# A new plan of pieces for VectorE in a three-stage image pipeline

## The chip, the cores and the metric

The kernel runs on one core of one Trainium2 chip. The time is device microseconds from start to end of the program, the median of three runs. The engines are TensorE (PE for its matmuls, PEld for its weight loads), VectorE (DVE), ScalarE (ACT), GpSimd (POOL) and SyncE (SP), which issues the transfers of the queue named q1.

## The reference

For 64 images of 64 channels by 64 by 64 pixels the reference computes three blocks, each with a residual.

```python
def reference(x, ...):
    h = _L0_tok_ref(x, ...)                                  # 16 pixels -> 1 token: 8-head attention in a 4x4 patch
    h = h + _L0_attn_ref(_layernorm(h, axis=-1), ...)        # selective scan forwards and backwards, gated
    h = h + _L0_ffn_ref(_layernorm(h, axis=-1), ...)         # product keys, then causal attention over 256 tokens
    return h

# the scan, 16 states for each of 128 channels
def step(h, inp):
    dA_t, dBu_t, c = inp
    h = dA_t * h + dBu_t
    return (h, jnp.einsum('bdn,bn->bd', h, c))

# the product keys: two lists of 64 scores for each of 8 heads
scores, idx = jax.lax.top_k(sim, PK_TOPK)                    # 16 best of each list
score = (scores[0][..., :, None] + scores[1][..., None, :])  # all pairs of the two lists
final_scores, pk_idx = jax.lax.top_k(score, FINAL_TOPK)      # 16 best pairs
k = jnp.einsum('bnhk,bnhkd->bnhd', softmax(final_scores), keys_table[ind])
v = jnp.einsum('bnhk,bnhkd->bnhd', softmax(final_scores), values_table[ind])
```

## The kernel before

Three images are in work at once. Each engine runs one loop body per image, and a body has 56 **slots** (`SLOTS`). In a period the engines do three things side by side: the third stage of image b (sums over the tables and attention), the second stage of image b+1 (product keys) and the first stage of image b+2 (patch attention and scan). The engines are tied by semaphores alone; a slot is a place in each engine's program and has no fixed length.

In every slot PE does the dense sums of image b: the exponents of the slot before (line 913), the count of entries over the limit (907), the product with a tile of the table for the slot two before (890, or 896 from slot 50 on). ACT turns the two into weights (line 1164 for the slot before, 1158 for this one), so PE and ACT hand work to each other once a slot. In the slots of `SUMS` PE adds four gathered groups (926); POOL gathers them from the table by indirect transfers (695) up to six groups ahead.

The attention of image b runs one head in seven slots: stage 0 (slots 0, 7, ..., 49) makes q on PE (940) and first waits for the accumulation of the head before on DVE; stage 2 makes v (949); stage 3 the scores (954 to 957), after which DVE takes the maxima (1731, 1732); stage 4 the exponentials on ACT (1196, 1197); stage 5 the transposes (961) and DVE's reciprocal (1735); stage 6 the output (965 to 967), which DVE adds into `acc` (1742).

All other work is cut into **pieces**, and a table of text says in which slot each engine issues a piece: `FIRST` for the first stage, `SECOND` for the second, `OWN` for what of the second stage runs over into the image's own period. `v.` is DVE, `p.` PE, `a.` ACT. Within a slot an engine issues the dense work, then attention, then the pieces of the second stage, then those of the first. The pieces that matter here:

- `T0` to `T19`, DVE: top 16 of the score lists, five steps for each of four groups of eight lists: maximum (1516), indices (1518), replace (1520), maximum (1522), indices (1524).
- `q0`, `q1`, `q2`, DVE (1392 to 1407): scores of the patch attention. ACT's piece `sc` in slot 20 (1064) waits for `q2`. `pv0` to `pv2` finish the patch attention.
- `L` and `G`: the same list steps on the pairs of scores. `pr0`, `pr1` make the pairs; `wd`, `wx`, `wg`, `wh` the softmax weights; `sel`, `selh` (1642 to 1648) mark the chosen pairs.
- `A`, `re`, `lo`, `e`: moved scores, their split in three parts, and one-hot counts. PE turns the counts (`e`, line 875, 16 matmuls), ACT copies them (1151).
- `R0` to `R9`, DVE (1610, 1613): table rows of one list of chosen pairs; each odd one also writes the rows for POOL (1619, 1621). `wb0` to `wb4` (1723) spread the weights.
- `B0` to `B3` (1465), `sf`, `sb` (1474), `C0` to `C3` (1484, 1485), DVE: the scan in four quarters: input, forward and backward scan, product with C and the first sums. `S0` to `S7`, PE (814): the state sums. S0 and S1 wait for C0, S2 and S3 for C1, and so on. `y` ends the scan.

The numbers behind `STORE_...` are SP's slots for the stores of the split scores.

Of the kernel before, what the change touches and what calls it, by code (L numbers as in the profile page):

```python
# [123 lines left out]
45 v.B3 v.sf3  # L124
46 v.sb3
47 v.C0
48 p.S0 v.C1
49 p.S1
50 p.S2 v.C2
51 p.S3 v.C3  # L130
52 p.S4
53 p.S5
54 p.S6
55 p.S7
56 p.y v.y
# [11 lines left out]
9 v.T0 v.T1  # L147
10 v.T2 v.T3 p.s1 a.s1
11 v.T4 v.T5 p.s2 a.s2
12 v.T6  # L150
13 v.T7 v.T8 p.s3 a.s3
14 v.T9 v.T10
15 v.T11
16 v.T12 v.T13
19 v.T14
20 v.T15 v.T16
23 v.T17 v.T18
24 v.T19 v.cp v.i a.cp
25 v.pr0 v.L0 v.L1
26 v.L2 v.L3  # L160
27 v.wd v.pr1
28 a.wd
29 v.wx v.sel v.A0 v.G0
30 a.ln p.A0 a.hi0
31 v.A1 v.G1
32 v.re0 v.e0 a.mi0
33 v.G2 p.A1 a.hi1
34 v.e1 v.lo0
35 v.G3 v.re1 a.mi1
36 v.lo1 p.e0 a.e0  # L170
37 v.G4 v.e2 p.e1 a.e1
38 v.wg v.e3 p.e2 a.e2
39 a.wg p.e3 a.e3
40 v.wh
41 a.l2
44 v.R2
46 v.R3
47 v.X5 v.wb0
49 v.R4 v.R5
50 v.A2 v.A3  # L180
51 v.selh
52 v.R6 v.R7
53 v.wb1 v.e4 p.A2 a.hi2
54 v.R8 v.re2 a.mi2
55 v.e5 v.lo2 p.e4 a.e4
"""

OWN = """
0 p.e5 a.e5
1 v.R9 v.e6 p.A3 a.hi3  # L190
2 v.re3 v.R0 v.lo3 a.mi3
3 v.e7 p.e6 a.e6
4 v.R1 v.wb2 v.wb3 p.e7 a.e7
10 v.wb4
"""


LOAD_X, STORE_OUT, STORE_2, STORE_3, STORE_0, STORE_BC = 13, 15, 1, 5, 40, 35
LOAD_C = (42, 44, 46, 48)


# [1630 lines left out]
```

## Time and profile before

| | us |
|---|---|
| median of 3 runs | 17549.33 |
| lowest, highest | 17534.83, 17637.0 |
| the profiled execution | 17614.6 |
| its span (first to last instruction) | 17612.8 |

| engine | busy us | share of the span |
|---|---|---|
| PE | 13397.9 | 76% |
| DVE | 10470.6 | 59% |
| POOL | 10063.1 | 57% |
| ACT | 7416.4 | 42% |

The mean granted TensorE clock is 0.823 of full speed. The span is 64 images, so 275 us an image with the fill and the drain in it. No engine is full, and what bounds the kernel changes from slot to slot. A row of the trace gives the start in us, the duration in us, the engine, the line, the operation, the tiles written and read, and in brackets how long the engine was idle before it and what ended that: an engine with its line, "issue" (nothing the profile shows), "remote" (an event that the profile can't place) or a DMA.

### The profile page before, as it was taken

To read this page: it belongs to the slowest core of one execution; us is meant where nothing else is said; L and a number is where in the kernel's file an instruction comes from. 1 tells how busy PE (TensorE), PEld (TensorE's weight loads), DVE (VectorE), ACT (ScalarE), POOL (GpSimd) and SP (SyncE) were. 2 spreads that over 40 slices of the span, in tenths; PEclk is the share of its full clock that TensorE was granted. 3 is DMA by queue.
4 is the path that set the end of the run, shared out by engine and by line. 5 is a ranking of instruction groups with operands and counts; after the bars stand their busy time and mean duration, and the time that the engine had idled before them with its cause. 6 is when DMAs were issued, how large, how long until landed. Compare 5 with 4: busy or idle time off the path is not lost.

```text
span 17612.8 us, 261382 instructions
## 1 busy us (share of the span) xinstructions
PE 13397.9 (76%) x71228; PEld 10390.9 (59%) x71228; DVE 10470.6 (59%) x39940; ACT 7416.4 (42%) x17286; POOL 10063.1 (57%) x9220
## 2 busy tenths in 40 slices
PE   4777777777777777777777778777777777777777
PEld 3656556556565555565656656556556665565565
DVE  6656656566566566565665656656656566566562
ACT  2444444444444444444444444444444444344443
POOL 2555555556556556555555556555655555556565
PEclk6888888888888888888888888888888788788888
DMA  2444434444444344343443444444434444344343
GB/s 80 115 114 113 114 108 115 118 110 119 114 112 118 108 115 122 107 116 109 116 117 107 118 111 120 117 113 116 116 108 117 115 112 116 105 116 122 107 116 95
DMA packets 1643030, 1984.06 MB, mean 113 GB/s; under 512 B 527806, under 2 KB 1129022, under 8 KB 1628990
## 3 DMA queue, kind: packets, MB, share of 16 engines
q1 hardware_dynamic: 1346366, 1359.69, 27.2%
q0 software_dynamic: 294912, 604.57, 13.2%
q8 instruction: 665, 10.90, 0.3%
q14 instruction: 1087, 8.90, 0.2%
HBM read 1898.00 MB, written 65.01 MB: 111 GB/s over the span
## 4 chain that ended last, share of the span: by engine, by line
PE 38%; another core or an unknown queue 20%; DVE 15%; issue 13%; ACT 8%; DMA 4%; SPq 1%; DVEq 0%; ACTq 0%
PE bank L890 9%; PE bank L926 6%; DMA moving<-keyspace 4%; PE bank L913 4%; ACT bank L1158 3%; PE bank L907 3%; PE bank L767 2%; PE bank L814 2%; PE bank L875 2%; ACT weight L1164 2%; PE bank L896 1%; PE bank L949 1%; PE bank L851 1%; DVE decay L1484 1%
## 5 line engine op out<-in xcount | busy, mean ns | idle before, releaser
L695 POOL DMA_INDIRECT gath<-in_table_dram,rowsT x9216 | 10062.9, 1092 | 7503.4 <-PE bank L926 3775.8
L890 PE MATMUL bank<-weight,rowtab 128*128 128x256 f32 x12288 | 3919.7, 450 | 0.0
L1164 ACT ACTIVATE weight<-bank 128x512 f32<-128x512 f32 x3584 | 2129.3, 594 | 2782.6 <-PE bank L913 1536.2
L890 PEld LDWEIGHTS bank<-weight,rowtab 128*128 128x128 f32 x12288 | 2814.0, 230 | 825.2 <-issue 196.6
L926 PEld LDWEIGHTS bank<-spread,gath 128*128 128x128 f32 x18432 | 2868.0, 223 | 202.3 <-issue 14.5
L913 PE MATMUL bank<-moving,pick_b 96*128 96x512 bf16 x3584 | 1583.5, 442 | 1730.9 <-ACT bank L1158 1282.0
L926 PE MATMUL bank<-spread,gath 128*128 128x96 f32 x18432 | 2773.9, 301 | 15.6 <-issue 15.3
L1158 ACT ACTIVATE bank<-bank,seventeen 128x512 f32<-128x512 f32 x3584 | 2379.1, 664 | 545.9 <-issue 408.5
L907 PE MATMUL bank<-moving,pick_b 96*128 96x512 bf16 x3584 | 1590.2, 444 | 420.4 <-DMA moving<-keyspace 256.4
L913 PEld LDWEIGHTS bank<-moving,pick_b 96*128 96x128 bf16 x3584 | 400.9, 112 | 2268.3 <-ACT bank L1158 1545.6
L1731 DVE TENSOR_REDUCE negmax<-bank 128x1 f32<-128x128 f32 x512 | 147.8, 289 | 2601.6 <-remote 1389.4
L1474 DVE TENSOR_TENSOR_SCAN decay<-decay,wide 128x1024 f32<-128x1024 f32 x512 | 1162.8, 2282 | 26.3
L1742 DVE SCALAR_TENSOR_TENSOR acc<-bank,rrow,acc 128x64 f32<-128x64 f32 x1024 | 245.3, 278 | 1553.2 <-issue 1080.4
L814 PE MATMUL bank<-decay,ident 128*128 128x256 f32 x2048 | 680.8, 461 | 506.7 <-DVE decay L1485 479.3
L767 PE MATMUL bank<-wkv,pix 128*128 128x130 f32 x4096 | 724.3, 328 | 379.9 <-issue 269.2
L767 PEld LDWEIGHTS bank<-wkv,pix 128*128 128x128 f32 x4096 | 616.1, 228 | 580.0 <-issue 450.9
L1089 ACT ACTIVATE decay<-delta,a_neg 128x255 f32<-128x255 f32 x2048 | 867.3, 503 | 1.7 <-DVE mx L1459 1.7
L814 PEld LDWEIGHTS bank<-decay,ident 128*128 128x128 f32 x2048 | 413.5, 224 | 619.5 <-DVE decay L1485 492.2
L1516 DVE MAX8 best<-sim 128x8 f32<-128x64 f32 x2048 | 281.6, 209 | 807.9 <-ACT sim L1111 785.2
L1054 ACT ACTIVATE wide<-bank 128x390 f32<-128x390 f32 (+1 forms) x768 | 346.3, 461 | 950.6 <-remote 779.3
L1709 DVE TENSOR_TENSOR onehot<-keys_b,idx_b 128x2048 bf16<-128x2048 bf16 x512 | 621.1, 1213 | 155.4 <-remote 136.5
L907 PEld LDWEIGHTS bank<-moving,pick_b 96*128 96x128 bf16 x3584 | 376.6, 105 | 568.6 <-DMA moving<-keyspace 274.7
(266 smaller groups left out, 20279.7 us busy)
## 6 DMA issues: line engine op xcount, KB each, us to landing
rowtab<-in_tableD_dram SPq DMA_DIRECT2D x2048, 256.0 KB
wide<-states SPq DMA_DIRECT2D x512, 512.0 KB
moving<-keyspace SPq DMA_DIRECT2D x3072, 64.0 KB
gath<-in_table_dram,rowsT POOLq DMA_INDIRECT x9216
moving<-keyspace SPq DMA_DIRECT2D x3072, 32.0 KB
pix<-in_x_dram SPq DMA_DIRECT2D x64, 1024.0 KB
pix<-in_x_dram SPq DMA_DIRECT2D x128, 512.0 KB
keyspace<-split SPq DMA_DIRECT2D x192, 256.0 KB, 2.0
```

The lines of the kernel that those rows point to most:

```text
L695: pool.indirect_dma_start(out=gath[:, u % RING, j, :], out_offset=None, in_=table, in_offset=bass.IndirectOffsetOnAxis(ap=rowsT[k][:, col: ...
L767: last = mm((scan_ps, misc)[c % 2][:, (n - n0) * KVW:(n - n0 + 1) * KVW], pix[:, n * TOK + t * P:n * TOK + (t + 1) * P], wkv[:], start=Tru ...
L814: mm(scan_ps[:, r * TOK:(r + 1) * TOK], ident[:], decay[r][:, n * TOK:(n + 1) * TOK], start=(n == 0 and r == 0), stop=False, skip_group_ch ...
L890: last = mm(dense_ps[:, 0:TOK], rowtab[:, r, s % 2 * 2 + half, :], weight[s % 2][:, half * TOK:(half + 1) * TOK], start=(s % 16 == 0 and h ...
L907: mm(zd_ps[s % 2][:], pick_b[:, 1, :], moving[r][:], start=True, stop=True, skip_group_check=True).then_inc(over_mm, 1)
L913: mm(zd_ps[s % 2][:], pick_b[:, 0, :], moving[s % KEY_RING][:], start=False, stop=True, skip_group_check=True).then_inc(z_ready, 1)
L926: last = mm(sums_ps[:, col:col + STREAM], gath[:, u % RING, j, :], flat[:, col:col + STREAM], start=True, stop=True)
L1089: last = af(decay[r][:, n * TOK + 1 - r:(n + 1) * TOK - r], delta[:, 1 - r:TOK - r], ACT.Exp, scale=a_neg[:, r * STATE + n:r * STATE + n + 1])
L1158: af(zd_ps[s % 2][:], zd_ps[s % 2][:], ACT.Relu, scale=-BIG, bias=seventeen[:, 0:1]).then_inc(over_ready, 1)
L1164: af(weight[s % 2][:], zd_ps[s % 2][:], ACT.Exp, scale=-1.0).then_inc(weight_ready, 1)
L1474: ins = v.tensor_tensor_scan(d, d, j, 0.0, ALU.mult, ALU.add)
L1709: ins = v.tensor_tensor(hot[:], keys_b[:].unsqueeze(1).to_broadcast([P, 2, KEYS, TOPK]), mine.unsqueeze(2).to_broadcast([P, 2, KEYS, TOPK] ...
```

## The change

Only the tables are changed, so every piece does what it did, in another slot. The diff, cut to the lines spoken of:

```diff
--- before.py
+++ after.py
@@ -124,12 +124,11 @@
 47 v.C0
-48 p.S0 v.C1
-49 p.S1
-50 p.S2 v.C2
-51 p.S3 v.C3
-52 p.S4
-53 p.S5
+48 v.C1
+50 p.S0 p.S1 v.C2
+51 p.S2 v.C3
+52 p.S3
+53 p.S4 p.S5
 54 p.S6
@@ -147,55 +146,55 @@
-19 v.T14
-20 v.T15 v.T16
+17 v.T15
+18 v.T16
+19 v.T17
+20 v.T18 v.T19 v.cp a.cp
...
-49 v.R4 v.R5
-50 v.A2 v.A3
-51 v.selh
-52 v.R6 v.R7
+49 v.wb1
+52 v.e4 v.R8 p.A2 a.hi2
...
-LOAD_X, STORE_OUT, STORE_2, STORE_3, STORE_0, STORE_BC = 13, 15, 1, 5, 40, 35
+LOAD_X, STORE_OUT, STORE_2, STORE_3, STORE_0, STORE_BC = 13, 15, 0, 4, 37, 35
```

All moves, as slots before -> after. DVE: T7 13 -> 12, T9 14 -> 13, T11 15 -> 14, T12 16 -> 15, T14 19 -> 16, T15 20 -> 17, T16 20 -> 18, T17 23 -> 19, T18 23 -> 20, T19 24 -> 20, i 24 -> 21, pr0 25 -> 22, L0 and L1 25 -> 23, L2 and L3 26 -> 24, wd 27 -> 24, pr1 27 -> 25, wx, sel and A0 29 -> 26, G0 29 -> 27, A1 and G1 31 -> 28, re0 and e0 32 -> 29, G2 33 -> 30, e1 and lo0 34 -> 31, G3 and re1 35 -> 32, lo1 36 -> 33, G4 37 -> 33, e2 37 -> 34, wg and e3 38 -> 34, wh 40 -> 36, R2 44 -> 36, R3 46 -> 37, X5 and wb0 47 -> 37, R4 49 -> 38, R5 49 -> 40, A2 50 -> 41, A3 50 -> 42, selh 51 -> 42, R6 52 -> 44, R7 52 -> 46, wb1 53 -> 49, e4 53 -> 52, R8 54 -> 52, re2 54 -> 53, e5 55 -> 53, lo2 55 -> 54, and of the own period R9 1 -> 54, e6 1 -> 55, re3 and R0 2 -> 1, e7 3 -> 2, R1, wb2 and wb3 4 -> 3. PE's and ACT's halves of these pieces move with them: PE's e0 to e3 from slots 36 to 39 to slots 33 to 36, A0 30 -> 27, A1 33 -> 30, A2 53 -> 52, A3 1 -> 0, e4 and e5 one slot forward, e6 and e7 from 3 and 4 to 2 and 3.

Line numbers below and in the changed kernel are one smaller from line 128 on. In the orders that follow a row is line, operation, tile written and tiles read, size, and how often.

On PE, around the first state sums, before (814 are the state sums, 913, 907, 890 the dense work of slot 49, 940 is attention stage 0, which waits for DVE's 1742):

```order
L967 MATMUL bank<-vo,probT 128x64
L809 REGISTER_ALU
L814 MATMUL bank<-decay,ident 128x256 x2
L912 REGISTER_ALU
L913 MATMUL bank<-moving,pick_b 128x512
L907 MATMUL bank<-moving,pick_b 128x512
L890 MATMUL bank<-weight,rowtab 128x256 x2
L940 MATMUL bank<-xT,wq_ffn 64x256
L814 MATMUL bank<-decay,ident 128x256 x2
```

and changed:

```order
L906 MATMUL bank<-moving,pick_b 128x512
L889 MATMUL bank<-weight,rowtab 128x256 x2
L939 MATMUL bank<-xT,wq_ffn 64x256
L911 REGISTER_ALU
L912 MATMUL bank<-moving,pick_b 128x512
L906 MATMUL bank<-moving,pick_b 128x512
L884 REGISTER_ALU
L895 MATMUL bank<-weight,rowtab 128x128 x4
L920 REGISTER_ALU
L925 MATMUL bank<-spread,gath 128x96 x4
L808 REGISTER_ALU
L813 MATMUL bank<-decay,ident 128x256 x4
```

The dense work of slot 49 now stands ahead of the first state sums, and so does attention stage 0; S0 and S1 stand together behind the sums of slot 50.

On DVE, from the accumulation of slot 48 on, before:

```order
L1742 SCALAR_TENSOR_TENSOR acc<-bank,rrow,acc 128x64 x2
L1484 TENSOR_TENSOR decay<-decay,wide 128x1024
L1485 TENSOR_TENSOR decay<-decay 128x512
L1484 TENSOR_TENSOR decay<-decay,wide 128x1024
L1485 TENSOR_TENSOR decay<-decay 128x512
L1610 TENSOR_TENSOR apart<-pair_row,fin_p 128x800
L1613 TENSOR_REDUCE row_f<-apart 128x16
L1610 TENSOR_TENSOR apart<-pair_row,fin_p 128x800
L1613 TENSOR_REDUCE row_f<-apart 128x16
L1619 SCALAR_TENSOR_TENSOR rowx<-row_f,headoff 128x32
L1621 STREAM_TRANSPOSE rowsT<-rowx 128x32
```

and changed:

```order
L1741 SCALAR_TENSOR_TENSOR acc<-bank,rrow,acc 128x64 x2
L1483 TENSOR_TENSOR decay<-decay,wide 128x1024
L1484 TENSOR_TENSOR decay<-decay 128x512
L1483 TENSOR_TENSOR decay<-decay,wide 128x1024
L1484 TENSOR_TENSOR decay<-decay 128x512
L524 REGISTER_ALU
L1722 TENSOR_TENSOR spread<-wT,own 128x256
L1483 TENSOR_TENSOR decay<-decay,wide 128x1024
L1484 TENSOR_TENSOR decay<-decay 128x512
```

The two row pieces R4 and R5 between C1 and C2 are gone from here; they now stand in slots 38 and 40.

On DVE, between the maxima of slot 17 and the end of `q2`, for which ACT waits, before:

```order
L1732 TENSOR_REDUCE negmax<-bank 128x1
L1392 COPY qs<-bank 128x144
L1394 TENSOR_TENSOR decay<-wide,qs 128x2048
L1399 TENSOR_REDUCE sc<-decay 128x256
L1735 RECIPROCAL rrow<-rowsum 128x2
L1524 MAX_INDEX best_i<-best,left 128x8 x8
L1402 TENSOR_TENSOR sc<-sc,rstd 128x256
L1403 TENSOR_TENSOR sc<-sc,qs 128x256
L1406 TENSOR_REDUCE mx<-sc 128x16
L1407 TENSOR_TENSOR sc<-sc,mx 128x256
```

and changed:

```order
L1515 MAX best<-sim 128x8 x8
L1391 COPY qs<-bank 128x144
L1393 TENSOR_TENSOR decay<-wide,qs 128x2048
L1517 MAX_INDEX best_i<-best,sim 128x8 x8
L1398 TENSOR_REDUCE sc<-decay 128x256
L1734 RECIPROCAL rrow<-rowsum 128x2
L1519 MATCH_REPLACE left<-best,sim 128x64 x8
L1401 TENSOR_TENSOR sc<-sc,rstd 128x256
L1402 TENSOR_TENSOR sc<-sc,qs 128x256
L1405 TENSOR_REDUCE mx<-sc 128x16
L1406 TENSOR_TENSOR sc<-sc,mx 128x256
```

Where one list step stood there are three: T15, T16 and T17 in place of T14.

## Rows read from the trace of the kernel before

**Rows 1.** The page's head: span, engines.

```profile
span 17612.8 us, 261382 instructions
PE 13397.9 (76%) x71228; PEld 10390.9 (59%) x71228; DVE 10470.6 (59%) x39940; ACT 7416.4 (42%) x17286; POOL 10063.1 (57%) x9220
```

**Rows 2.** Groups over the whole run: count | busy us, mean ns | idle us before, releasers.

```profile
L814 PE MATMUL bank<-decay,ident 128*128 128x256 f32 x2048 | 680.8, 461 | 506.7 <-DVE decay L1485 479.3 <-issue 26.9
```

**Rows 3.** Stretches, slots 31-38, 38-45, 48-52: length, busy PE PEld DVE ACT POOL, granted clock.

```profile
8067.30:8105.30 38.00, 28.31 (x145) 22.11 (x143) 17.97 (x95) 15.35 (x38) 16.56 (x18) 0.77 0.42 124
8105.30:8133.80 28.50, 24.20 (x137) 19.48 (x136) 22.67 (x24) 21.01 (x53) 22.79 (x17) 0.83 0.53 170
8147.10:8166.30 19.20, 17.97 (x91) 13.29 (x92) 18.62 (x37) 6.40 (x13) 15.55 (x12) 0.86 0.46 116
```

**Rows 4.** Timeline, PE, slots 48 and 49.

```profile
8147.06 2.08 PE L814 MATMUL bank<-decay,ident 128*128 128x256 f32 x4 [6.40 <-DVE decay L1485]
8148.93 0.63 PE L913 MATMUL bank<-moving,pick_b 96*128 96x512 bf16 x1
8151.62 1.05 PE L940 MATMUL bank<-xT,wq_ffn 64*64 64x256 f32 x2
8152.60 1.13 PE L814 MATMUL bank<-decay,ident 128*128 128x256 f32 x4
```

**Rows 5.** Timeline, DVE, the waits of slots 38, 41 and 45, and slot 48.

```profile
8105.27 0.29 DVE L1731 TENSOR_REDUCE negmax<-bank 128x1 f32<-128x128 f32 x1 [7.78 <-PE bank L957]
8117.10 0.48 DVE L1742 SCALAR_TENSOR_TENSOR acc<-bank,rrow,acc 128x64 f32<-128x64 f32 x2 [2.30 <-issue]
8133.77 0.29 DVE L1731 TENSOR_REDUCE negmax<-bank 128x1 f32<-128x128 f32 x1 [2.87 <-PE bank L957]
8146.92 0.47 DVE L1742 SCALAR_TENSOR_TENSOR acc<-bank,rrow,acc 128x64 f32<-128x64 f32 x2
```

**Rows 6.** Groups over the whole run, DVE: the pieces R (two rows), e.

```profile
L1613 DVE TENSOR_REDUCE row_f<-apart 128x16 f32<-128x800 f32 x640 | 630.9, 986 | 22.0
L1610 DVE TENSOR_TENSOR apart<-pair_row,fin_p 128x800 f32<-128x800 f32 x640 | 627.7, 981 | 17.1
L1709 DVE TENSOR_TENSOR onehot<-keys_b,idx_b 128x2048 bf16<-128x2048 bf16 x512 | 621.1, 1213 | 155.4 <-remote 136.5 <-PE bank L875 10.4 <-issue 8.4
```

**Rows 7.** Stretches, DVE busy: slots 38 to C0; A2, A3, selh; wg, wh, X5, wb0.

```profile
8105.20:8147.00 41.80, 35.62 (x43) 0.83 0.55 169
sum 1.94, DVE 1.83; mean DVE 0.92
sum 2.40, DVE 2.20; mean DVE 0.73
```

**Rows 8.** Groups over the whole run: own period and slot 27, ACT.

```profile
L1142 ACT ACTIVATE split_h<-rest 128x128 bf16<-128x128 f32 x64 | 19.8, 310 | 127.9 <-issue 102.6 <-DVE rest L1684 24.9
L1037 ACT ACTIVATE lnv<-var 128x34 f32<-128x34 f32 (+1 forms) x128 | 27.0, 211 | 154.5 <-DVE var L1436 87.1 <-issue 61.2 <-DVE var L1383 6.2
```

**Rows 9.** Groups over the whole run: sc on ACT, the list steps on DVE.

```profile
L1064 ACT ACTIVATE sc<-sc 128x256 f32<-128x256 f32 x64 | 26.6, 416 | 185.7 <-issue 111.8 <-DVE sc L1407 73.9
L1518 DVE FIND_INDEX8 best_i<-best,sim 128x8 uint32<-128x64 f32 x2048 | 411.2, 220 | 117.9 <-issue 117.2
L1516 DVE MAX8 best<-sim 128x8 f32<-128x64 f32 x2048 | 281.6, 209 | 807.9 <-ACT sim L1111 785.2 <-issue 22.8
```

**Rows 10.** Timeline: T16 on DVE (first, last of 16 rows), ACT meanwhile.

```profile
8009.47 0.09 DVE L1518 MATCH_VALUE_LOAD best_i<-best,sim 128x8 f32 x1 [1.25 <-DVE best L1516]
8015.21 0.22 DVE L1518 FIND_INDEX8 best_i<-best,sim 128x8 uint32<-128x64 f32 x1
8015.32 0.38 ACT L1190 ACTIVATE qT<-bank 64x256 f32<-64x256 f32 x1 [7.03 <-remote]
```

**Rows 11.** Groups over the whole run: e2 and e3 on PE; the copies of e on ACT.

```profile
L875 PE MATMUL bank<-down_b,onehot 128*128 128x128 bf16 x2048 | 168.3, 242 | 66.4 <-ACT split L1151 52.1 <-issue 9.4 <-DVE onehot L1709 3.5
L1151 ACT ACTIVATE split<-bank 128x128 bf16<-128x128 f32 x384 | 105.9, 276 | 849.7 <-remote 560.2 <-PE bank L875 248.7 <-issue 38.7
```

More of the change, by code:

```diff
@@ L149 @@
 11 v.T4 v.T5 p.s2 a.s2
[L150 to L154, printed above, removed]
-19 v.T14
-20 v.T15 v.T16
[L157 to L178, printed above, removed]
-49 v.R4 v.R5
-50 v.A2 v.A3
-51 v.selh
-52 v.R6 v.R7
-53 v.wb1 v.e4 p.A2 a.hi2
-54 v.R8 v.re2 a.mi2
-55 v.e5 v.lo2 p.e4 a.e4
+12 v.T6 v.T7
+13 v.T8 v.T9 p.s3 a.s3
+14 v.T10 v.T11
+15 v.T12
+16 v.T13 v.T14
+17 v.T15
+18 v.T16
+19 v.T17
+20 v.T18 v.T19 v.cp a.cp
+21 v.i
+22 v.pr0
+23 v.L0 v.L1
+24 v.L2 v.L3 v.wd
+25 v.pr1 a.wd
+26 v.wx v.sel v.A0
+27 v.G0 a.ln p.A0 a.hi0
+28 v.A1 v.G1
+29 v.re0 v.e0 a.mi0
+30 v.G2 p.A1 a.hi1
+31 v.e1 v.lo0
+32 v.G3 v.re1 a.mi1
+33 v.lo1 v.G4 p.e0 a.e0
+34 v.e2 v.wg v.e3 p.e1 a.e1
+35 a.wg p.e2 a.e2
+36 v.wh v.R2 p.e3 a.e3
+37 v.R3 v.X5 v.wb0 a.l2
+38 v.R4
+40 v.R5
+41 v.A2
+42 v.A3 v.selh
+44 v.R6
+46 v.R7
+49 v.wb1
+52 v.e4 v.R8 p.A2 a.hi2
+53 v.re2 v.e5 a.mi2
+54 v.lo2 v.R9 p.e4 a.e4
+55 v.e6 p.e5 a.e5
 """
 OWN = """
[L189 to L193, printed above, removed]
+0 p.A3 a.hi3
+1 v.re3 v.R0 a.mi3
+2 v.lo3 v.e7 p.e6 a.e6
+3 v.R1 v.wb2 v.wb3 p.e7 a.e7
 10 v.wb4
 """
-LOAD_X, STORE_OUT, STORE_2, STORE_3, STORE_0, STORE_BC = 13, 15, 1, 5, 40, 35
+LOAD_X, STORE_OUT, STORE_2, STORE_3, STORE_0, STORE_BC = 13, 15, 0, 4, 37, 35
 LOAD_C = (42, 44, 46, 48)
```

## The prediction

> **What bounds the kernel now.** I read the page's head first, then the groups with their idle time, then one period by stretches, then its timeline where an engine waits long. The reader is to see in the head that no engine comes near the span [rows 1]: PE 76%, DVE and POOL under 60%. So this is a kernel of hand-overs, and which engine ends a wait last has to be asked place by place. All figures below are us per image unless another unit stands there.
>
> In slots 31 to 38 DVE works 17.97 of 38.00, and PE is busy 28.31; from slot 38 to 45 DVE works 22.67 of 28.50, and from slot 48 to 52 it works 18.62 of 19.20 [rows 3]. DVE is thus the engine waited for from about slot 45 to slot 52 and has room before. The clearest sign is PE's state sum S0: it stands in slot 48 behind C0 and waits 6.40 for it [rows 4]; over the run those waits are 479.3, so 479.3 / 64 = 7.5 an image [rows 2]. POOL's rows and gathers are not waited for there. The second place where DVE is waited for is slot 20: ACT's `sc` sits idle 185.7 / 64 = 2.9 until `q2` is through [rows 9]. Before slot 38 it is the other way round: DVE waits 7.78 for the scores of PE [rows 5].
>
> **The change part by part.** It adds and removes no arithmetic and no transfer; it moves pieces. Six places count, each per image.
>
> 1. *Slots 38 to 47, until C0.* Moved in: R4 to R7, moved out: R2 and R3, so two row pieces more at 0.981 + 0.986 = 1.97 each [rows 6], 3.94, with one more writing of rows, about 0.4. Moved out too is e3, 1.21 [rows 6]. Of the small pieces A2, A3 and selh come in with 1.94, and wg, wh, X5 and wb0 leave with 2.40 [rows 7]. Net 3.94 + 0.4 - 1.21 + 1.94 - 2.40 = +2.7 of DVE work. The stretch is 41.80 long with 35.62 busy [rows 7], so DVE would need 38.3 without a wait. It does wait, in slot 41 for 2.30 and in slot 45 for 2.87 [rows 5], for PE; PE loses e2 and e3 there (168.3 / 64 = 2.6 [rows 11]), so it comes sooner. Bounds: 0 if the waits stay, -3.5 if all go. I take the middle, **-1.7** for the end of C0.
>
> 2. *S0 to slot 50.* In slot 49 PE waits at attention stage 0 for DVE's accumulation of slot 48, which starts in DVE's order right behind C0 (8146.92, against S0's 8147.06) [rows 4, 5]. So the wait does not go, it changes its name. What is won is the dense work of slot 49: from 8148.93 to 8151.62, 2.7, which PE now does inside the wait [rows 4]. Behind the wait the clock was at the lower level: S0 took 2.08 where the next sums took 1.13 [rows 4]. A pause shorter by 2.7 may cost less of this; bounds 0 and -1.6 (the 0.95 of S0 and some 0.65 of the dense work behind it, by the same ratio), I take -0.8. On the other side PE's A3 comes ahead of `y`, +0.4 at most (a piece of 2 matmuls against the 16 of an e, 1.3 [rows 11]). Sum **-3.1**, bounds -4.3 and 0 (0 if DVE, not PE, sets slot 52). DVE would not: of its 18.62 in slots 48 to 52 [rows 3] R4, R5, A2, A3 and selh leave (3.94 + 0.4 + 1.94 = 6.3).
>
> 3. *Own slots 0 to 4.* R9 and e6 no longer stand ahead of re3, for which ACT's split_h waits 127.9 / 64 = 2.0 [rows 8]. Bounds -2.0 and 0; I take **-1.4**, since PE has the same work to do there.
>
> 4. *Slots 17 to 20.* Between the maxima of slot 17 and the end of `q2` there is now T15, T16, T17 instead of T14: a maximum of 281.6 / 256 = 1.1 and an index step of 411.2 / 256 = 1.6 more [rows 9], 2.7 together. `sc` waits already, so this lies on the path whole, unless a later wait swallows it: right behind, in slot 21, ACT stood 7.03 in a wait called "remote" [rows 10]. Bounds 0 and +2.7; I take **+2.0**.
>
> 5. *Slots 24 to 32.* With T19, pr0 and the first lists gone from slots 24 and 25, `h1` comes sooner, and ACT's wait at 1037 (154.5 / 64 = 2.4 [rows 8]) falls by about 1. In slot 32 ACT's copy for side 1 now stands behind G3, ten maxima at the pace of [rows 9], 1.3, and a subtraction: +1.5. Together **+0.5**, bounds -2.4 and +1.7.
>
> 6. *Slots 33 to 38.* e2 and e3 come in from slots 38 and 39: PE 2.6, and each has a copy on ACT of 0.28, which waited 849.7 / 384 = 2.2 [rows 11]. PE and ACT bound this stretch, since DVE waits 7.78 at its end [rows 5]. Some falls into waits that are there. Bounds 0 and +4; I take **+2.0**.
>
> The store slots 37, 0 and 4 follow the pieces; SP has nothing more to issue and waits there for copies one slot old, as before. I put it at nothing; if a copy came late, the key loads behind it would be late next.
>
> The sum is -1.7 - 3.1 - 1.4 + 2.0 + 0.5 + 2.0 = -1.7. Of 64 images some 61 run in the full pipeline, so -104. From the profiled execution, 17614.6, it gives 17511. That execution is 65 over the median of the three runs, 17549.33; taken off the median, which is what I forecast, it is **17445** (-0.6%). All bounds at their low end are -3.5 - 4.3 - 2.0 + 0 - 2.4 + 0 = -12.2, at the high end 0 + 0 + 0 + 2.7 + 1.7 + 4 = +8.4 (16805 and 18062); terms of different places will not all end on one side.
>
> For the clock in part 2, the page "TensorE: Matmul & The Clock Gate" of the Trainium skill (section "What's actually happening") says that the default state is the throttled one and that activity releases it. A pause of 3 to 4 us would stay in front of attention stage 0, and by that rule the work behind it may still be slow. The low clock behind the pause of 6.40 agrees with it [rows 4]. With no gain of clock the sum would be -0.9 an image, 17494.
>
> **The rivals.** *The added work hides.* ACT's waits called "remote" are long: 7.03 before 1190 in slot 21 [rows 10] and 560.2 / 64 = 8.8 an image before the copies of e [rows 11]. If they end at a time that the pieces ahead do not move, then part 4 costs nothing and part 6 only 0.5: -1.7 - 2.0 - 1.5 = -5.2, times 61 = -317, so 17232 (-1.8%). For it speaks their size; against it that I cannot say what they wait for. The page "Runtime: NRT & Kernel Launch" of the Trainium skill (section "Instruction fetch mechanics") has instruction fetch mostly hidden behind running work, which would speak against such waits being fetch; no row here decides.
>
> *Slow lists in front of q2.* T16's index step, 1.6 on average, took from 8009.47 to 8015.21 here, 5.7 plus, because its instructions came in steps of 0.7 [rows 10]. Today this costs little, since `q2` is already through. In the change T16 and T17 stand in front of `q2`. If they keep this pace there, each costs 3.6 more (7.2 together): -1.7 + 7.2 = +5.5, times 61 = +336, so 17885 (+1.9%). It decides from an extra of 4.6 (then +2.9, +1%). Against it: T14, in the very place between q1 and q2, ran quickly, or the wait of `sc` would be longer than 2.9 [rows 9].
>
> *S0's move does nothing.* The wait at attention stage 0 takes all: part 2 is 0, the sum +1.4, +85, so 17634 (+0.5%). The order and the numbers of part 2 speak against it, since the 2.7 of slot 49 does run inside the wait.
>
> **How the numbers follow.** A measurement of this kernel tells about 1% from no change. My forecast, with the likeliest sum, has 0.31. "The added work hides" has 0.25, and I give 0.08 more to gains over 1% from parts 1 and 2 at their better ends. "S0's move does nothing" has 0.14. Slow lists have 0.14, and 0.08 goes to part 6 at its worse end with little won in part 1. So faster by over 1%: 0.33; within 1%: 0.31 + 0.14 = 0.45; slower by over 1%: 0.14 + 0.08 = 0.22. The range reaches from a little below 17232 to between the 17634 of the third case and the 17885 of the second: 17180 to 17780, which leaves out about 0.1 on each side.
>
> **What would show it.** Right: PE's idle time before 814 nearly gone, and in its place a wait of 3 to 4 before 940 in slot 49, ended by DVE's accumulation; DVE's maxima of slot 52 some 4 to 5 sooner after those of slot 38; the wait of split_h below 1; `sc` waiting over 5. Wrong: the wait before 940 as long as the 6.40 of S0 with C0 no sooner (parts 1 and 2); `sc` waiting as before (part 4); T16 or T17 several us long in front of `q2` (the second rival); stretches 31 to 38 longer by over 4 (part 6). The forecast fails altogether if the waits called "remote" grow where the order has changed, for nothing in the rows tells what sets them.

## The result, and the profile after

| | before | after |
|---|---|---|
| median of the runs | 17565.36 us (4 runs) | 18000.25 us (4 runs, 17984.6 to 18028.71) |
| ratio | | 1.0233, 95% interval 1.0214 to 1.0252 |
| profiled execution | 17614.6 us | 17984.6 us |
| one image, slot 0 to slot 0, mean of 59 | 272.0 us | 277.7 us |

The change made the kernel 2.3% slower. The forecast was 0.6% faster, 17445 us, with a range up to 17780: both its sign and its range were wrong. The page of the kernel after, its head and the groups that answer to [rows 1, 2, 8, 9, 11] (lines after 128 are one lower than before):

```profile
span 17982.8 us, 261638 instructions
PE 13440.4 (75%) x71228; PEld 10390.2 (58%) x71228; DVE 10464.2 (58%) x39940; ACT 7441.1 (41%) x17286; POOL 10222.6 (57%) x9220
L813 PE MATMUL bank<-decay,ident 128*128 128x256 f32 x2048 | 608.2, 430 | 114.3 <-DVE decay L1484 80.3 <-issue 32.6
L939 PE MATMUL bank<-xT,wq_ffn 64*64 64x256 f32 x1024 | 383.6, 460 | 551.5 <-DVE acc L1741 450.1 <-issue 101.1
L1141 ACT ACTIVATE split_h<-rest 128x128 bf16<-128x128 f32 x64 | 19.7, 308 | 88.1 <-DVE rest L1683 88.1
L1063 ACT ACTIVATE sc<-sc 128x256 f32<-128x256 f32 x64 | 26.6, 416 | 256.3 <-issue 159.9 <-DVE sc L1406 96.4
L1036 ACT ACTIVATE lnv<-var 128x34 f32<-128x34 f32 (+1 forms) x128 | 26.7, 209 | 11.0 <-DVE var L1382 7.9 <-DVE var L1435 2.8
L1150 ACT ACTIVATE split<-bank 128x128 bf16<-128x128 f32 x384 | 106.4, 277 | 1256.3 <-remote 1013.6 <-PE bank L874 232.9 <-issue 9.8
L694 POOL DMA_INDIRECT gath<-in_table_dram,rowsT x9216 | 10222.4, 1109 | 7714.5 <-PE bank L925 4158.3 <-issue 2631.5 <-remote 685.7
```

No engine has more instructions than before; POOL's 9216 gathers take 10222.4 us instead of 10063.1. PE's idle time before the state sums has nearly gone (506.7 before, 114.3 now), and the wait has its new name at L939, as forecast. Before, that line had read:

```profile
L940 PE MATMUL bank<-xT,wq_ffn 64*64 64x256 f32 x1024 | 375.1, 451 | 241.3 <-issue 151.1 <-DVE acc L1742 83.9 <-remote 5.8
```

What grew is ACT's wait before the copies of `e`, from 849.7 to 1256.3, and within it the part called "remote", from 560.2 to 1013.6.

Where in the image does the time go? The slots are marked by the start of ACT's activation for the count over the limit (L1158, in the changed kernel L1157), one in each slot. The difference of their lengths, after minus before, mean of 59 images, summed from slot 0:

| up to the end of slot | 4 | 16 | 20 | 23 | 32 | 38 | 45 | 48 | 52 | 53 | 54 | 55 |
|---|---|---|---|---|---|---|---|---|---|---|---|---|
| after minus before, us | -0.5 | +1.0 | +2.8 | +1.2 | -0.4 | -3.3 | -5.2 | -11.6 | -6.8 | -3.6 | +5.2 | +5.7 |

By the end of slot 52 the change is 6.8 us an image ahead; the forecast was 1.7 for the whole image. Slots 53 and 54 take 12 us, more than the whole gain. In one image there, by stretches (length, busy PE, PEld, DVE, ACT, POOL with their instructions, granted clock, DMA share, GB/s), the first three beside [rows 3]:

```profile
8226.40:8262.40 36.00, 27.40 (x165) 21.76 (x166) 18.65 (x67) 17.58 (x44) 16.42 (x16) 0.83 0.49 147
8262.40:8288.90 26.50, 20.68 (x116) 16.20 (x116) 25.91 (x36) 19.93 (x47) 21.84 (x14) 0.97 0.46 138
8302.00:8316.20 14.20, 14.20 (x72) 11.36 (x73) 11.10 (x13) 4.11 (x8) 11.77 (x8) 0.78 0.53 145
8316.20:8323.80 7.60, 7.60 (x57) 6.81 (x55) 7.46 (x9) 2.78 (x8) 6.07 (x6) 1.00 0.32 91
8323.80:8344.00 20.20, 8.67 (x36) 5.64 (x34) 2.79 (x7) 1.64 (x3) 13.23 (x14) 0.62 0.19 54
```

In the last stretch PE, DVE and ACT work 8.67, 2.79 and 1.64 us out of 20.20, and the DMA engines are busy 19%. Only POOL goes on, gather after gather. The timeline of POOL, ACT, DVE and PE there:

```profile
8323.76 0.95 POOL L694 DMA_INDIRECT gath<-in_table_dram,rowsT  x1 [0.30 <-issue]
8325.02 0.99 POOL L694 DMA_INDIRECT gath<-in_table_dram,rowsT  x1 [0.31 <-issue]
...
8340.05 0.94 POOL L694 DMA_INDIRECT gath<-in_table_dram,rowsT  x1 [0.30 <-issue]
```

```profile
8325.10 0.66 ACT L1157 ACTIVATE bank<-bank,seventeen 128x512 f32<-128x512 f32 x1
8333.47 0.49 ACT L1200 ACTIVATE probT<-bank 128x384 f32<-128x384 f32 x1 [7.70 <-remote]
8344.06 0.28 ACT L1150 ACTIVATE split<-bank 128x128 bf16<-128x128 f32 x1 [10.10 <-remote]
8344.38 0.47 DVE L1741 SCALAR_TENSOR_TENSOR acc<-bank,rrow,acc 128x64 f32<-128x64 f32 x2 [17.70 <-remote]
```

```profile
8323.27 0.49 PE L960 MATMUL bank<-ident,prob 128*128 128x128 f32 x3
8325.31 0.44 PE L874 MATMUL bank<-ident_b,onehot 128*128 128x128 bf16 x4 [0.33 <-issue]
...
8336.25 0.27 PE L965 MATMUL bank<-vo,probT 128*128 128x64 f32 x1 [0.23 <-issue]
...
8337.66 0.26 PE L966 MATMUL bank<-vo,probT 128*128 128x64 f32 x1 [1.14 <-issue]
...
8344.48 1.90 PE L874 MATMUL bank<-ident_b,onehot 128*128 128x128 bf16 x16 [5.63 <-ACT split L1150]
```

Here the reader is to see three things. ACT's copy `probT` (L1200) needs the transposes of PE's L960, done at 8323.8, and starts at 8333.5; the copy at L1150 needs the sums of e4, done by 8325.8, and starts at 8344.1. So these waits end long after the work that they wait for: that is what "remote" means here. PE meanwhile issues about one matmul every 0.7 us. And all of it starts again 3 us after POOL's last gather of a row of 14, 1.25 us apart (0.94 of work, 0.30 of issue).

Is that one image, or a rule? I call a run of gathers that start under 1.6 us apart a train, and took the busy share of each engine in the 1.2 us behind the start of each gather, by its place in the train (worked out from the records of 59 images):

| place in the train | before: PE, DVE, ACT | after: PE, DVE, ACT |
|---|---|---|
| 1st | 0.82, 0.80, 0.56 | 0.82, 0.84, 0.56 |
| 4th | 0.83, 0.53, 0.27 | 0.83, 0.46, 0.30 |
| 6th | 0.55, 0.29, 0.13 | 0.58, 0.35, 0.17 |
| 8th | 0.42, 0.19, 0.12 | 0.40, 0.11, 0.11 |
| 10th | 0.12, 0.29, 0.07 | 0.16, 0.13, 0.03 |
| 13th | none | 0.09, 0.01, 0.02 |

So the kernel before has it too: trains of 8 or more come 7 times an image there (423 in 59 images), but only 10 of them had over 10 gathers. After the change 53 had 13 or more, and 45 of these start in slot 53 or 54: such a train in three images of four. The experiments ask whether the trains cause the standstill or only go along with it, and why the change made this one.

### The profile page after: what moved, and what is told of

It is laid out like the page before. It is cut to its first block, busy times and chain, and to the rows that moved or that the text cites. A ratio compares the mean times of both kernels' runs of the same rounds, so it can differ in the third digit from the quotient of the medians.

```text
span 17982.8 us, 261638 instructions
## 1 busy us (share of the span) xinstructions
PE 13440.4 (75%) x71228; PEld 10390.2 (58%) x71228; DVE 10464.2 (58%) x39940; ACT 7441.1 (41%) x17286; POOL 10222.6 (57%) x9220
## 4 chain that ended last, share of the span: by engine, by line
PE 32%; DVE 22%; another core or an unknown queue 18%; issue 17%; ACT 6%; DMA 4%; SPq 1%; DVEq 0%; ACTq 0%
PE bank L889 6%; PE bank L925 5%; DMA moving<-keyspace 4%; PE bank L766 3%; PE bank L912 2%; PE bank L906 2%; ACT bank L1157 2%; PE bank L813 2%; PE bank L895 2%; DVE decay L1473 2%; PE bank L874 2%; DVE wide L1464 2%; DVE apart L1609 1%; ACT weight L1163 1%
## 5 line engine op out<-in xcount | busy, mean ns | idle before, releaser
L694 POOL DMA_INDIRECT gath<-in_table_dram,rowsT x9216 | 10222.4, 1109 | 7714.5 <-PE bank L925 4158.3
L889 PE MATMUL bank<-weight,rowtab 128*128 128x256 f32 x12288 | 3809.8, 440 | 2.7 <-issue 2.5
L889 PEld LDWEIGHTS bank<-weight,rowtab 128*128 128x128 f32 x12288 | 2744.5, 224 | 778.0 <-issue 175.0
L925 PEld LDWEIGHTS bank<-spread,gath 128*128 128x128 f32 x18432 | 2859.0, 223 | 212.5 <-issue 35.1
L925 PE MATMUL bank<-spread,gath 128*128 128x96 f32 x18432 | 2772.3, 301 | 29.9 <-issue 29.5
L1157 ACT ACTIVATE bank<-bank,seventeen 128x512 f32<-128x512 f32 x3584 | 2381.3, 664 | 481.0 <-issue 391.4
L1473 DVE TENSOR_TENSOR_SCAN decay<-decay,wide 128x1024 f32<-128x1024 f32 x512 | 1172.3, 2290 | 26.5 <-issue 0.2
L874 PE MATMUL bank<-ident_b,onehot 128*128 128x128 bf16 x6144 | 564.2, 251 | 624.8 <-ACT split L1150 466.6
L874 PEld LDWEIGHTS bank<-ident_b,onehot 128*128 128x128 bf16 x6144 | 498.6, 153 | 677.7 <-issue 671.8
L939 PE MATMUL bank<-xT,wq_ffn 64*64 64x256 f32 x1024 | 383.6, 460 | 551.5 <-DVE acc L1741 450.1
L895 PEld LDWEIGHTS bank<-weight,rowtab 128*128 128x128 f32 x4096 | 655.8, 225 | 191.0 <-issue 126.9
```

The lines of the kernel that those rows point to most:

```text
L694: pool.indirect_dma_start(out=gath[:, u % RING, j, :], out_offset=None, in_=table, in_offset=bass.IndirectOffsetOnAxis(ap=rowsT[k][:, col: ...
L874: last = mm(big_b[:, t * P:(t + 1) * P], hot[:, :, r], down_b[:, r, :] if side == 1 else ident_b[:], start=(r == 0), stop=(r == TOPK - 1))
L889: last = mm(dense_ps[:, 0:TOK], rowtab[:, r, s % 2 * 2 + half, :], weight[s % 2][:, half * TOK:(half + 1) * TOK], start=(s % 16 == 0 and h ...
L895: last = mm(dense_ps[:, 0:P], rowtab[:, r, q, :], weight[s % 2][:, q * P:(q + 1) * P], start=(s % 16 == 0 and q == 0), stop=(s == SLOTS - ...
L925: last = mm(sums_ps[:, col:col + STREAM], gath[:, u % RING, j, :], flat[:, col:col + STREAM], start=True, stop=True)
L1157: af(zd_ps[s % 2][:], zd_ps[s % 2][:], ACT.Relu, scale=-BIG, bias=seventeen[:, 0:1]).then_inc(over_ready, 1)
```

## The experiments

Theory G: gathers issued close together on POOL hold up the other engines. Rival D: the standstill comes from the density or the supply of instructions. Rival P: it comes from the pieces e4 to e6 waiting for each other. The edits are shown cut to the line that differs. Each ratio is to the kernel before, run beside it on the same chip. Five chips were used. The kernel before took 17332 and 17345 us on two of them and 17565 to 17596 on the other three, so times from different chips are not compared, only their ratios. Whether a ratio is the same on both kinds of chip was not tested, so small differences between ratios of different chips are not ranked.

### Half the gathers

```
-                    for j in range(PART):
+                    for j in range(0, PART, 2):
```

> The changed kernel with every second gather of GpSimd left out (2 of 4 per part; the sums read the other two twice, so the gathered values are wrong, all other work is there). Theory G (gathers): a train of back-to-back gathers on GpSimd holds up PE, ACT and DVE, and the change lost its gain in slots 53 and 54 to a train of 14. With trains at most half as long nearly all waits called remote should go, 272 us an image should fall to 235 or less, about 15500 us or less, and the changed order should come out 1.5 to 2.5% faster than the order of before under the same cut. Theory D (density of instructions, or their supply): the other engines' instructions are the same, so the stalls stay: 17700 to 18000 us, and still 2% over the kernel before. Theory P (the pieces e4 to e6 wait for each other's data in slots 53 to 55): the same as D.

> The kernel before with every second gather of GpSimd left out, as in the other run (its gathered values are wrong). Theory G: 15800 us or less, and 1.5 to 2.5% over the changed order with the same cut. Theories D and P: 17400 to 17600 us, 2% under the changed order with the same cut.

Measured: changed order 14052.72 us, 0.8101 (0.8085 to 0.8118); order of before 14143.9 us, 0.8154 (0.8137 to 0.8171). ACT's copies of `e` in the changed order with half the gathers:

```profile
L1150 ACT ACTIVATE split<-bank 128x128 bf16<-128x128 f32 x384 | 106.6, 278 | 445.8 <-PE bank L874 428.3 <-remote 13.6 <-issue 3.4
```

The same 384 copies waited 1013.6 us "remote" in the change; here 13.6. What is left of the wait is for PE, at its true name. Both orders lose 18 to 19% of their time, though PE, ACT and DVE have the same instructions. D and P, which expected no gain, fall. G had said about 15500 us or less, a gain of some 11%; it is 19. And the changed order is now the faster one, by 14052.72 / 14143.9, that is 0.6%. G had said 1.5 to 2.5%, so the order alone is worth less than I read from slot 52.

### The gathers held to PE's slots

All gathers are done, but POOL waits before each pair until PE has come within L slots of the sum that reads it (L - 1 for the second pair). The ring of six parts by itself lets POOL go 9 slots ahead.

```
+                        if j % 2 == 0:
+                            wait(pool, dense_done, b * SLOTS + SUMS[g][u % 8] - L + j // 2 - 1)
+                            pool.sem_inc(held, 1)
                         pool.indirect_dma_start(
```

> The changed kernel, all its gathers done, but GpSimd may issue each pair of gathers only once PE is 6 (second pair of a part: 5) slots from the sum that reads them, so it cannot run ahead in a train of 14. Theory G: the train of slots 53 and 54 becomes pieces of 2 to 4, the stall of 18 us there falls to under 8, and the time to 17400 to 17650 us, with most of the waits called remote shorter. Theories D and P: 17950 to 18100 us, since neither the instructions nor the data dependences of the other engines change (or slower, if gathers now come late).

> The kernel before with GpSimd's gathers held to PE's slots as in the run gate_after (6 and 5 slots ahead of the sum). Theory G: trains are cut here too, 3 to 4% below the kernel before. It also tells what the change of pieces is worth once the trains are short: by the sum of the prediction (1.7 us an image) the changed order with the hold is 0.6% faster than this run, so this run stands at 0.969 of the kernel before where gate_after stood at 0.963; rival: the order is worth nothing by itself, 0.960 to 0.965; rival: without the hold the change made slots 53 and 54 denser, and that costs with it too, under 0.960.

> The changed kernel with the hold one slot looser (7 and 6 slots ahead instead of 6 and 5). With the hold at 6 PE waited 206 us for gathered rows in all. If that lateness is now what costs more than trains: 0.955 to 0.962 of the kernel before. If short trains still decide: 0.965 to 0.985, with more gathers in trains of 6 and more than the 38% of gate_after.

> The kernel before with the hold of 7 and 6 slots. Stands beside gate8_before for the width of the hold. Theory G: 0.930 to 0.945 of the kernel before.

> The kernel before with the hold of 8 and 7 slots, close to what the ring of six parts allows by itself (9 slots). Theory G: the looser the hold, the longer the trains: 0.945 to 0.975, over gate7_before. If only the start of a part in two halves counts and not how far GpSimd may run: the same as gate7_before.

> The changed kernel with the hold of 8 and 7 slots, on the same chip as gate8_before, so the ratio of the two is the worth of the changed order with shorter trains. By the sum of the prediction 0.994; by the runs with half the gathers (218.2 and 216.9 us an image) also 0.994; if the changed order still meets a longer train in slots 53 and 54: 1.005 to 1.02.

| run | L | order | ratio, 95% interval | trains of 8 or more in 59 images |
|---|---|---|---|---|
| before | none | before | 1 | 423 |
| after | none | changed | 1.0233 (1.0214 to 1.0252) | 407, of these 53 of 13 or more |
| gate_after | 6 | changed | 0.9634 (0.9592 to 0.9677) | 145 |
| gate_before | 6 | before | 0.9387 (0.9365 to 0.9409) | 151 |
| gate7_after | 7 | changed | 0.9359 (0.9335 to 0.9383) | 170 |
| gate7_before | 7 | before | 0.9457 (0.9427 to 0.9487) | 154 |
| gate8_after | 8 | changed | 0.9402 (0.9369 to 0.9435) | 125 |
| gate8_before | 8 | before | 0.942 (0.9389 to 0.945) | 112 |

A hold on POOL, which adds a wait and takes nothing away, makes either order 4 to 6% faster. D and P had said 17950 to 18100 us for gate_after and G 17400 to 17650; it took 16735.8, so G had the way right and the size wrong. Nor did the ratios of gate_before and gate7_after come out as I had expected (0.969, or 0.960 to 0.965, against 0.9387, and 0.955 to 0.985 against 0.9359). My expectation that a looser hold brings the trains and the time back was wrong: L = 8, one slot short of the ring's own limit, has no more long trains than 6, and gate8_before is no slower than gate7_before. The hold does not end all trains: those of six or more are 635 in gate8_before and 520 before, but those of eight or more fell from 423 to 112. Why gate_after lags gate_before I can't say; they ran on different chips, and at both L = 6 and L = 7 the lower ratio is the one from a chip on which the kernel before is slow. So I don't rank the three widths. Of the same width, only gate8_after and gate8_before ran on one chip: 16275.6 against 16326.42 us, 0.3% for the changed order, with intervals that overlap.

### The hold on the first parts alone

```
+                        if j % 2 == 0 and u < 6:
```

(L = 6, for the parts that POOL issues from slot 50 on.)

> The changed kernel with the hold on the first 6 parts of an image's gathers only, those that GpSimd issues from slot 50 on into the next image; all others run as in the change. If the train of 14 in slots 53 and 54 alone lost the gain there (8.8 us in slot 54): 6 to 10 us an image less than the change, 0.985 to 1.000 of the kernel before. If those stalls come from something else that the hold everywhere only happened to relieve: over 1.015. If the stall only moves to the next train: 1.000 to 1.015.

Measured: 0.9941 (0.9924 to 0.9959), 2.9% under the change. Slot 54 fell from 14.58 to 7.04 us and slot 53 from 8.52 to 4.30. So this one train is what turned a gain into the loss. Part of it only moved: POOL now makes up its gathers in slots 3 to 6 of the next image, in one train of 17 (timeline of ACT):

```profile
7868.79 0.20 ACT L1106 ACTIVATE rstdb<-lnvb 128x2 f32<-128x2 f32 x1
7880.13 0.88 ACT L1056 ACTIVATE wide<-bank 128x390 f32<-128x390 f32 x2 [11.14 <-remote]
```

### The instructions of the hold without the hold; whole parts

```
null_after:    - 20 in place of - L (a wait that is always met)
whole8_after:  if j == 0   (L = 8, four gathers at a time)
```

> The changed kernel with the same wait and semaphore step before each pair of gathers as in gate8_after, but 20 slots back, so that it is always met: the instructions are there, the hold is not. Theory G1 (a train does harm because GpSimd runs ahead of PE's slots): as without, 1.015 to 1.03 of the kernel before. Theory G2 (it does harm because its gathers are issued with nothing between them; a short pause between pairs is enough): 0.93 to 0.96, as gate8_after.

> The changed kernel with the hold of 8 slots before a whole part of four gathers only, none between its pairs. Theory G1: 0.95 to 0.98, nearly all of the gain of gate8_after (0.940). Theory G2: 0.98 to 1.02, since four gathers follow each other without a pause and half of the pauses are gone. If both count, between.

Measured: null_after 1.0308 (1.0273 to 1.0343), whole8_after 0.9788 (0.9755 to 0.982). So the gain does not come with the added instructions; it needs the hold to PE's slots (G1). But G2 is tested only in part: in null_after the gathers start 1.249 us apart at the median, as in the change, so its instructions make no pause. A real pause between pairs, without a tie to PE, was not tried. Four at a time keep 4.5 points of the gain over the change, two at a time (0.9402) give 8.3. Their trains of 8 or more: 481, 360 and 125. I had expected nearly the whole gain from whole parts; that was too much.

### Bytes, rows or number of gathers

```
narrow_after:  in_=table.rearrange("r (h c) -> (r h) c", h=2)   (64 numbers a row, not 128)
rows64_after:  out=gath[0:64, u % RING, j, :]                   (64 rows, not 128)
```

> The changed kernel with as many gathers, each fetching 64 of a row's 128 numbers (after the first image; the gathered values are wrong). If it is the bytes of the gathers that hold the others up, the stalls shrink about as with half the gathers: 0.81 to 0.92 of the kernel before. If it is the number of gathers or of their rows, issued back to back, whatever they carry: 1.00 to 1.03, and trains of 6 or more still have the dead time beside them.

> The changed kernel with as many gathers, each of 64 rows instead of 128 (after the first image; the lower half of the gathered rows is stale and so wrong). Halving the bytes of a row had left the time as it was (1.019). If the stall goes by the number of gathers: 1.00 to 1.03. If it goes by rows, that is by what GpSimd writes for each row: 0.82 to 0.95, with each gather shorter than its 1.11 us.

Measured: 1.0191 (1.0158 to 1.0225) and 1.016 (1.013 to 1.0191). POOL's gathers in the second:

```profile
L695 POOL DMA_INDIRECT gath<-in_table_dram,rowsT x9216 | 9886.5, 1073 | 7933.5 <-PE bank L926 4115.4
```

Half the rows make a gather shorter by 3% (1109 to 1073 ns) and leave the standstill: the place in the train counts, not what a gather carries (PE busy 0.46 at the 8th gather, 0.40 in the change).

### One part of the change alone, and its tail undone

```
sums_only (from before):   48 p.S0 / 49 p.S1 / ... / 53 p.S5   ->   50 p.S0 p.S1 / 51 p.S2 / 52 p.S3 / 53 p.S4 p.S5
tail_back (from after):    pieces of slots 49 to 55 and own 0 to 4 as before
```

> The kernel before with nothing changed but PE's state sums, S0 to S7 in slots 50 to 55 as in the change. By part 2 of the prediction alone: 3.1 us an image less (of it 0.8 of clock), 0.989 of the kernel before, bounds 0.985 to 1.000. By theory G: the same gain up to slot 52, but PE now reaches the sums of gathered rows in slots 50 to 54 close together, frees the ring faster and lets GpSimd run on: part or all of it lost in slots 53 to 55, 0.995 to 1.01.

> The changed kernel with the pieces of slots 49 to 55 and of the image's own slots 0 to 4 back in the slots of before (wb1, e4, e5, A2 on PE, R8, R9, re2, lo2, A3 on PE, stores at 1 and 5), the state sums in slots 50 to 55 and everything before slot 49 as changed. If the loss sits in these pieces (theories D and P, or G by way of earlier rows R8 and R9): 17250 to 17500 us. If it sits in the sums S0 to S7 alone, or if PE, arriving earlier at slot 52, sets off the same train whatever DVE does (theory G): 17800 to 18000 us.

sums_only: 0.9894 (0.9861 to 0.9927). Part 2 of the prediction gives 0.989; theory G's 0.995 to 1.01 was missed. The agreement with part 2 is in part luck. Its profile (on a chip on which the kernel before, too, was 1.6% faster than in its own profile, some 4 us an image) is 5.5 us ahead of before's between the end of slot 38 and that of slot 52, and slots 53 to 55 take 5.7 back. Much of both is work that has only moved: PE is busy 3.0 us less in slots 48 to 52 and 4.1 more in slots 53 to 55. From C0 to DVE's maxima of slot 52, where part 2 put its 3.1, it gains only 1.2, and 3.2 come in slots 0 to 4. It has no train over 12. tail_back: 1.0077 (1.0053 to 1.0101); it was expected at 17250 to 17500 us if the tail's pieces carried the loss, and took 17480.95. But as a ratio it is still over 1: slots 53 to 55 cost 9.3 us in it, where they cost 12.4 in the change. By these stretches, which are from different chips, R8, R9 and the e pieces account for about a quarter of the loss there; by the ratios (1.0233 and 1.0077) the tail is worth some 4 us an image, nearer to a third. The rest comes from what happens earlier.

How far POOL lags tells what. This is the number of gathers that the ring would allow and that are not issued yet, at the start of a slot, mean of 53 images (worked out from the records of the gathers and from the plan, which counts the sums of all earlier slots as done):

| slot | 38 | 45 | 48 | 50 | 52 |
|---|---|---|---|---|---|
| before | 0.0 | 4.5 | 8.8 | 2.7 | 5.0 |
| sums_only | 0.2 | 4.6 | 9.4 | 6.6 | 8.6 |
| tail_back | 1.1 | 7.8 | 11.0 | 8.1 | 11.2 |
| after | 0.9 | 7.8 | 11.3 | 8.3 | 11.6 |

Before, PE's wait for S0 made slot 48 13.6 us long, and by slot 50 POOL had come from 8.8 down to 2.7. The change took this wait away (slot 48 is 4.8 us now) and filled DVE from slot 38 on: DVE's busy time there is 25.91 of 26.50, against 22.67 of 28.50 [rows 3]. Beside DVE's scans and products POOL is slow. In the change a gather took 0.94 us where DVE was idle at its start, 2.09 where a scan (L1473) was running and 1.57 where a product (L1483) was, means of 3451, 502 and 502 gathers. So POOL reaches slot 52 with 11.6 gathers owed, the scan's last products end, and the rest goes out at 1.25 us: the train of 14. sums_only, which takes only the wait away, owes 8.6 at slot 52; that is 3.6 of the 6.6 by which the change exceeds before. That the other half comes from the fuller DVE is argued from the table, and no run fills DVE and keeps the wait. The debt alone does not fix the loss either: tail_back owes 11.2, has 71 trains of 13 or more, and loses less.

### Versions that beat both

> The kernel before with only the state sums moved, as sums_only (0.989), and the hold of 8 and 7 slots (0.942 on the order of before). If the two add up: 0.930 to 0.934, better than the whole change with the hold. If the hold already takes what the sums' move gave: 0.940 to 0.945.

> The order of tail_back (the change with the pieces of slots 49 to 55 and 0 to 4 as before) with the hold of 8 and 7 slots. tail_back stood 1.5% under the change without the hold; with the hold slots 53 and 54 have no long train to save, so theory G expects less of it: 0.930 to 0.940. If the density of the pieces themselves cost time: 0.925 or less.

> As gate8_sums, but each single gather held to PE's progress: the first and third of a part to the start of a slot (PE's exponents), the second and fourth to its middle (PE's product). The step from whole parts to pairs gave 4% (0.979 to 0.940); if the stall grows with the number of gathers that PE lets go at a time, single ones give 1 to 3% more: 0.905 to 0.925 of the kernel before. If two at a time are short enough to do no harm, or the gathers now come late: 0.930 to 0.945.

```
each8_sums:  before every gather   wait(pool, (z_ready, dense_done)[j % 2],
                 b * SLOTS + SUMS[g][u % 8] - 8 + j // 2 - j % 2)
```

gate8_sums 0.934 (0.9308 to 0.9372), gate8_tail 0.9342 (0.9309 to 0.9374), each8_sums 0.9311 (0.929 to 0.9331). The two gains of gate8_sums, 0.942 and 0.9894, do add up (0.932 expected from them), though they come from another chip. gate8_tail and gate8_sums are equal: with the hold the other moved pieces add nothing to the sums' move. Single gathers gave at most 0.3% over pairs, not 1 to 3%. each8_sums has the lowest ratio of this study, though its interval overlaps gate8_sums': it has the table of before with the sums' rows changed and one wait before each gather, and is 6.9% faster than the kernel before. Its head:

```profile
span 16387.8 us, 273946 instructions
```

## Why the prediction was wrong, point by point

The prediction's own bounds cut the image into stretches: slots 0 to 4, 17 to 20, 24 to 32, slot 33 to DVE's maxima of slot 38, these to C0, C0 to the maxima of slot 52. Measured are the means of 53 images, changed order minus order of before, in the full kernel and in the two runs with half the gathers, where no train is longer than 4. (Over the 59 images above the full kernel's sum is +5.7.)

| part of the prediction | forecast (bounds) | full kernel | half the gathers |
|---|---|---|---|
| 1, maxima of slot 38 to C0 | -1.7 (-3.5 to 0) | -2.7 | -0.4 |
| 2, C0 to maxima of slot 52 | -3.1 (-4.3 to 0) | -4.8 | -3.8 |
| 3, slots 0 to 4 | -1.4 (-2.0 to 0) | -0.3 | -2.9 |
| 4, slots 17 to 20 | +2.0 (0 to +2.7) | +1.7 | +2.6 |
| 5, slots 24 to 32 | +0.5 (-2.4 to +1.7) | -1.5 | -0.9 |
| 6, slot 33 to maxima of slot 38 | +2.0 (0 to +4) | +0.9 | +3.2 |
| slots 5 to 16 and 21 to 23 | none | +0.1 | +0.7 |
| maxima of slot 52 to slot 0 | none | +12.9 | +0.3 |
| sum | -1.7 | +6.4 | -1.1 |

*Parts 1 and 2* gave more than forecast in the full kernel. Most of part 1's 2.7 hangs on the standstills: with half the gathers the stretch gives 0.4, with the hold of 8 it gives 0.3. Part 2 was right in mechanism, and holds up in both (3.8 and 3.9), but it needs DVE's moves too, since sums_only gives 1.2 there. PE waits at attention stage 0 in slot 49 for DVE's accumulation, and S0's wait has gone:

```profile
8301.96 1.08 PE L939 MATMUL bank<-xT,wq_ffn 64*64 64x256 f32 x2 [5.90 <-DVE acc L1741]
```

The wait is 5.90 here, where I forecast 3 to 4. The 0.8 of clock inside part 2 can't be found: the granted clock from this wait to slot 52 is 0.78, against 0.86 from S0 to slot 52 before [rows 3]. By the rule of the Trainium skill that the prediction cites, the work behind a remaining pause may still be slow; the trace agrees, with the granted clock at its lower level, 1.2 GHz, from 8298.1, inside the wait, to 8308.4.

*Part 3.* split_h's wait fell from 127.9 to 88.1 (2.0 to 1.4 an image; I had said below 1). With half the gathers the stretch gives 2.9. In the change slot 3 alone took 3.1 us more and ate most of it.

*Part 4* was right to 0.3, but `sc` waits 256.3 instead of 185.7, which is 4.0 an image and not "over 5". Slots 21 to 23 gave 1.3 back. What came in besides the maximum is the replace step T17, not an index step, at the same price (1.66). The rival of slow lists did not occur: T16 took 1.67 in the change. By its own numbers its price was too low, since 5.7 less 1.6 is 4.1 and not 3.6.

*Part 5* was inside its bounds. ACT's wait at 1036 fell by 2.2 (154.5 to 11.0 over the run), not 1.

*Part 6* was inside its bounds. The rival "the added work hides" gave it 0.5 and the full kernel shows 0.9; but with half the gathers the work of e2 and e3 costs 3.2, so what hid it were standstills.

*The step that failed* is one that the prediction did not have as a term. Its second paragraph says that POOL's rows and gathers "are not waited for there", and from that it costs POOL at nothing. Nobody waits long for a gather's data, that is true (PE idles 29.9 us before L925 in the whole run); but how POOL's gathers fall together sets whether the others run. The six terms came to -1.7 an image. Measured up to the maxima of slot 52 it was -6.5; then +12.9 to the image's end, for the most part from a train of gathers: with the hold on that train alone the same order stands 2.9% lower. The wait that part 2 counted as pure gain had been POOL's time to catch up. Taking it away alone made no train over 12; together with the fuller DVE it did. With half the gathers the order was worth -0.64%, and with the hold of 8 -0.3%, where the intervals overlap; the forecast was -0.6%. That this comes so near is luck in part: with half the gathers part 1 gives a quarter of its term, part 3 lies outside its bounds (-2.9, bound -2.0), part 6 costs 1.2 more than forecast, and the errors cancel. The prediction's last sentence named the place: that it fails altogether if the waits called "remote" grow. They did, from 560.2 to 1013.6 before the copies of `e` alone. I had seen them, 8.8 us an image, said that I could not tell what they wait for, and gave their growth no price and no chance. The range should have carried it. All views needed were there: the timeline of T16 [rows 10], whose steps of 0.7 us I took for a property of the list step, lies in a stretch with 9 gathers in a row (8002.10 to 8013.02), as most of the ACT wait of 7.03 does.

## What to carry to other kernels

A wait whose releaser the profile cannot name, and that ends long after the work it waits for, is to be laid against the timeline of every engine, the one nobody waits for too. A wait that is removed may have been the time in which another engine made up its arrears: count what that engine owes at the place before and after. Where one engine issues gathers whenever buffers are free, tie them to the consumer's progress, one or two at a time; here this was worth 6%, ten times what the moved pieces could give.

## What the runs showed of the hardware that was not expected

- Indirect gathers issued by POOL 1.25 us apart slow the other engines from about the fifth on: PE busy 0.83 at the 4th, 0.55 at the 6th, 0.12 at the 10th. It does not go by bytes (half of them: 1.019 against 1.023) nor by rows (half: 1.016). Half as many gathers: 0.810. The DMA engines are not the limit, 19% busy in the standstill.
- What is held up is not shown. Instructions start late on PE, ACT, DVE and SP alike, and packets of instructions are absent from 8316.1 to 8345.1 and then come in a burst, 9 within 6 us. Over 59 images of the change such packets start at 0.080 a us beside the first five gathers of a train of 8 or more, at 0.023 from the ninth on, and at 0.20 from 4 to 7 us after its end. That could be the cause or follow from engines that stand still. Nor is the place in a train all of it: with the hold of 8 PE was busy 0.77 at the 6th gather, against 0.55 before. The shares hold ordinary waits too: in the changed order with half the gathers PE was busy 0.20 at the 4th place of 176 trains, where it mostly waited for a key load, for ACT or for DVE's accumulation. An experiment that moves the gathers to other DMA queues was not tried.
- What a gather takes depends on what DVE is running when the gather starts. In the change it took 0.94 us where DVE was idle (3451 gathers) and also where the reduction of the row pieces ran (L1612, one input; 377). It took 2.09 where a scan ran (L1473, 502 gathers), 1.57 where a product ran (L1483, 502) and 1.32 where the subtraction of the row pieces ran (L1609, 245); these three read two inputs from SBUF. Such a gather ends a fixed time after DVE's instruction does, however much of that instruction was left: 0.75 us after a scan, 0.82 after a product or a subtraction (of each kind, nine in ten lie within 0.02 us). The Trainium skill ("SBUF — State Buffer", section "Who interferes with whom") says that a DVE instruction with two SBUF inputs contends with a GpSimd instruction that reads SBUF. The trace agrees: 2.09, 1.57 and 1.32 against 0.94. The same section has PE and ACT never waiting on anyone. That is said of ports; in the trains both stood still, PE at 0.09 and ACT at 0.02 at the 13th gather, so a kernel's plan can't rest on it.
